# Splitting the third weight unit of the last attention projection while the queries are applied

## The reference

```python
qkv = (x @ W_qkv).reshape(b, n, 3, H, DH)
...
q_p = _phi(q, random_features)        # exp(q . features - |q|^2 / 2) / sqrt(M)
k_p = _phi(k, random_features)
kv = jnp.einsum('bhnm,bhnd->bhmd', k_p, v)
out = jnp.einsum('bhnm,bhmd->bhnd', q_p, kv)
k_sum = jnp.sum(k_p, axis=2)
normalizer = jnp.einsum('bhnm,bhm->bhn', q_p, k_sum)[..., None]
out = out / (normalizer + 1e-06)
x_attn = out_as_rows @ W_proj + b_proj
y = x + x_attn
mu = jnp.mean(y, axis=-1, keepdims=True)
var = jnp.mean(jnp.square(y - mu), axis=-1, keepdims=True)
return (y - mu) * jax.lax.rsqrt(var + LN_EPS) * gamma + beta
```

## Time and profile before

| | before |
|---|---|
| median of three runs | 2881.58 us |
| the profiled execution's own time | 2884.14 us |
| span of its instructions | 2881.9 us |
| PE busy | 2717.6 us (94% of the span) |
| DVE busy | 1397.7 us (48%) |
| ACT busy | 1144.1 us (40%) |
| POOL busy | 712.7 us (25%) |
| mean granted clock of TensorE | 0.977 of full |

### The profile page before, as it was taken

The page is one execution under the profiler, slowest core; times in us unless marked ns, Lnnn a source line. Parts: engine busy times, 40 slices in busy tenths (PEclk is TensorE's granted clock), DMA queues, the critical chain, the costliest instruction groups (busy, mean ns, idle before and its releaser), DMA issues. The chain is left out here.

```text
span 2881.9 us, 49194 instructions
## 1 busy us (share of the span) xinstructions
PE 2717.6 (94%) x20011; PEld 2474.0 (86%) x20011; DVE 1397.7 (48%) x3595; ACT 1144.1 (40%) x2131; POOL 712.7 (25%) x265
## 2 busy tenths in 40 slices
PE   9999999998678999998899999999998999999899
PEld 9999999996338988998897999999668897797799
DVE  9777465665122134558742552241664473303643
ACT  7633255651004203328631263332563442356431
POOL 0134211100002321320224343323204341113022
PEclk9999999999799999999999999999999999999999
DMA  2022231025992111221031222222002121101112
GB/s 66 12 78 81 78 105 39 18 94 198 413 397 83 61 45 44 67 81 41 12 89 39 67 67 78 78 67 77 28 1 56 50 79 43 58 24 35 34 45 71
DMA packets 169682, 223.22 MB, mean 77 GB/s; under 512 B 22051, under 2 KB 150720, under 8 KB 169209
## 3 DMA queue, kind: packets, MB, share of 16 engines
q1 hardware_dynamic: 169458, 220.07, 23.3%
HBM read 216.56 MB, written 3.48 MB: 76 GB/s over the span
## 5 line engine op out<-in xcount | busy, mean ns | idle before, releaser
L284 POOL TENSOR_TENSOR weights_r<-weights,head_weights_r 128x1536 fp32r<-128x1536 f32 (+1 forms) x78 | 278.2, 3566 | 1061.6 <-ACT head_weights_r L277 1048.2
L58 PE MATMUL ps<-weights_r,buf_r 128*125 128x256 f32 (+2 forms) x3794 | 510.7, 285 | 5.2 <-POOL weights_r L284 1.9
L284 POOL TENSOR_TENSOR weights_r<-weights,weights_r 128x1536 fp32r<-128x1536 f32 (+1 forms) x74 | 262.3, 3545 | 914.1 <-ACT weights_r L277 914.1
L58 PEld LDWEIGHTS ps<-weights_r,buf_r 128*125 128x125 f32 x3794 | 478.2, 187 | 8.3 <-issue 3.5
L58 PE MATMUL ps<-head_weights_r,buf_r 128*125 128x256 f32 (+3 forms) x2548 | 351.6, 284 | 0.0
L58 PE MATMUL ps<-xT_r,weights_r 128*128 128x376 f32 (+3 forms) x2016 | 329.9, 309 | 0.0
L58 PEld LDWEIGHTS ps<-head_weights_r,buf_r 128*125 128x125 f32 (+1 forms) x2548 | 326.0, 187 | 0.0
L58 PEld LDWEIGHTS ps<-xT_r,weights_r 128*128 128x128 f32 x2016 | 304.1, 191 | 0.0
L58 PE MATMUL ps<-weights_r,xT_r 128*125 128x256 f32 x1680 | 232.1, 282 | 1.7 <-DVE resid L2380 0.9
L277 ACT ACTIVATE head_weights_r<-weights 128x1536 fp32r<-128x1536 f32 (+1 forms) x78 | 115.9, 1486 | 270.6 <-PE ps L58 158.8
L58 PEld LDWEIGHTS ps<-weights_r,xT_r 128*125 128x125 f32 x1680 | 212.4, 186 | 3.2 <-PE ps L2311 1.4
(11 more groups left out here) (419 smaller groups left out, 4369.6 us busy)
## 6 DMA issues: line engine op xcount, KB each, us to landing
expert_regions<-in_L_ffn_w SPq DMA_DIRECT2D x64, 576.0 KB, 12.9
expert_regions<-in_L_ffn_w SPq DMA_DIRECT2D x36, 768.0 KB, 20.8
weights<-in_L_mix_fc_w SPq DMA_DIRECT2D x24, 768.0 KB, 4.5
weights<-in_L_gnn_W SPq DMA_DIRECT2D x18, 768.0 KB, 4.6
expert_regions<-in_L_ffn_w SPq DMA_DIRECT2D x24, 384.0 KB, 9.6
weights<-in_L_ffn_W SPq DMA_DIRECT2D x11, 768.0 KB, 4.8
weights<-in_L_mix_w_mapT SPq DMA_DIRECT2D x9, 768.0 KB, 4.8
weights<-in_L_gnn_W_out SPq DMA_DIRECT2D x9, 768.0 KB, 4.6
```

Source lines behind the costliest of these rows:

```text
L58: mm = net.nc.tensor.matmul(ps, net.r(stationary(s, k)), net.r(moving(m, k)), start=(n == 0 and k == 0), stop=(stop and n == 2 and k == kc ...
L284: self.nc.gpsimd.tensor_tensor(self.r(load.dst), load.dst, self.r(load.high), ALU.subtract).then_inc(self.low_made, 1)
```

## The change

The third unit's high part goes into columns 3072 to 4607 of the edge buffer, and that place counts as free from `attended` on. The split moves from `LinearResidualNorm` into `QueryApply`: ACT writes the high part just before the entry `("high", 0, 1)` of its order, and POOL makes the low part in `QueryApply.gpsimd`. `LinearResidualNorm.gpsimd` does nothing now. `queried.third` hands the load to the earlier stage.

```diff
@@ QueryApply.__init__
+        self.third = None
@@ QueryApply.scalar
         for q in self.order["act"]:
             kind, c, j = q[0], q[1], q[-1]
             ts, n = self.halves(j)
+            if q == ("high", 0, 1):
+                self.net.split_high(self.third.unit, self.third.segment)
             if kind == "phi":
@@ QueryApply
+
+    def gpsimd(self, pool):
+        self.net.split_low(self.third.unit, self.third.segment)
@@ LinearResidualNorm.scalar
         nc, done, eps = self.nc, self.net.act, self.net.eps[self.eps][:TP, :]
-        self.net.split_high(self.weights[-1].unit, self.weights[-1].segment)
         for q in self.order["act"]:
@@ LinearResidualNorm
     def gpsimd(self, pool):
-        self.net.split_low(self.weights[-1].unit, self.weights[-1].segment)
+        pass
@@ network
-    normed = LinearResidualNorm(net, XT, units, tok(G[5]), net.row(ins["L3_mix_gamma"]), R, tok(G[0]), XT, 1e-5, G[3], now(), now() + bias_out.ends() + shift.ends(),
+    normed = LinearResidualNorm(net, XT, units, tok(G[5]), net.row(ins["L3_mix_gamma"]), R, tok(G[0]), XT, 1e-5, net.spare[:, 2 * SLOT:3 * SLOT], attended, now() + bias_out.ends() + shift.ends(),
                                 tiles=queried.made, partly=queried.partly)
+    queried.third = normed.weights[-1]
```

## The result

The changed kernel takes 2867.92 us (median of four runs, 2866.37 to 2870.05), the kernel before 2881.98 us beside it (2881.34 to 2884.27). The ratio is 0.995 with a 95% interval of 0.9933 to 0.9968: faster by 14.1 us, or by 9 to 19 us.

What follows compares the result with a forecast made beforehand. PE, busy 94% of the span, bounds the kernel; its 8.2 us wait and close to 1.9 us of low clock make 10.14 us gained, 0 paid: 2881.58 to 2871.4 us, range 2868.3 to 2874.8 us (8 in 10).

Steps and rivals of the forecast that it cites:

- The hole: PE's wait before its seventh ahead block, on POOL's low part, goes; sixth chunks start 10.14 us earlier, 8.2 of it wait.
- The second term, the low clock: Behind PE's wait, 3.80 us at half clock do the work of 1.90 us; close to 1.9 us gained.
- ACT's split covered: In `QueryApply`, ACT's moved split of 1.47 us fits its idle time of 1.90 us; none on the path.
- The side remark: Without ACT's idle time in `QueryApply`, exponentials would be late by up to 1.47 us once, and PE with them.
- POOL: The low part, 3.42 us, moves behind the ten additions, from about 2650.1 to 2653.5 us; none on POOL's path.
- DVE's hold: DVE's remainder of 250 tokens in `QueryApply` is held 1.7 to 3.6 us, about 3.2, by the low part; covered.
- the additions' hold: In `QueryApply`, a DVE remainder of 375 tokens took 2.23 us in place of 0.55 beside POOL's additions: held 1.7 us.
- The rule of the lock: DVE with two SBUF inputs and POOL reading SBUF block each other fully; remainder would end at about 2653.9 us.
- The range: Whole-kernel time, 8 in 10: 2868.3 to 2874.8 us, taking in the clock's two sides and DVE's full hold.
- The clock falls elsewhere: Low-clock stretches behind the change may fall otherwise: 3.4 us better, 2868.0, or as much worse, 2874.8 us; chance 0.08.

Runs made afterwards that it cites:

- Experiment 3: The kernel before with 60 unused matmuls on PE in the hole ahead of the third unit; ratio 0.9995 (0.9985 to 1.0004).
- experiment 4: The changed kernel's new place and early mark kept, but ACT splits at the old point; ratio 1.0003 (0.9994 to 1.0012) to the kernel before.
- experiment 7: The changed kernel with a second, unused copy of the unit on ACT ahead of the split; sixth chunks 61.40 us after the start of `QueryApply`.
- Experiments 5 and 6: The changed kernel with the split two and four pairs of heads later; sixth chunks 62.70 and 61.40 us after the start of `QueryApply`.

## Why the prediction was right, and where it was wrong

- **The hole.** Right to 0.02 us: 10.14 us forecast, 10.16 us in the pair of profiles; 10.2, 10.7 and 11.0 us against the three profiles of kernels with the hole (17.36, 17.93 and 18.22, less 7.20). Experiment 3 shows the split into two terms, experiment 4 that the moment of the split is the cause.
- **The second term, the low clock.** Right in kind; 1.8, 2.4 and 2.7 us in three profiles, where the sum has 1.9 from the only one that was there. By the blocks' starts the two terms of that profile are 8.34 us (2693.20 less 2684.86) and 1.80; the forecast's 8.2 and 1.9 are rounded otherwise, with the same sum.
- **ACT's split covered.** Right: 0.52 us of the gap were left, and the exponentials wait for PE as before. The side remark that without the cover PE would be late by as much as the exponentials was wrong: with the gap overrun the exponentials started 0.75 us late, ran closer together, ended 0.23 us late, and cost PE nothing that shows (experiment 7).
- **POOL.** Right: 2644.26 us in this profile, 22.8 us after the start of `QueryApply`, where 2650.1 in the old one was 22.9.
- **DVE's hold.** Right in size (3.2 us forecast, 3.2 measured) and right that the place hides it. Experiments 5 and 6 show that this is a property of the place: it costs PE some 1.3 us two pairs later and 0.2 us four pairs later. What the forecast missed is that the additions' hold of 1.7 us, taken from the one profile that it had, is 5.2 us in two profiles of twelve. Even then PE lost only 0.2 us.
- **The rule of the lock.** The Trainium skill ("SBUF — State Buffer", section "Who interferes with whom") says that the loser blocks for the whole instruction. In all three profiles above the held DVE instruction ends 0.3 to 0.4 us after POOL's: 2647.98 and 2647.71 us, 2671.84 and 2671.56, 2684.24 and 2683.84. By that rule the cost can be estimated before the run, within 0.2 us here: the end of POOL's instruction, plus the instruction's own time. It holds for a single POOL instruction. Against the additions, which follow each other without a gap, the loser waited for one of them in ten profiles and for three in two.
- **The range: wrong.** The step that failed is the rival "The clock falls elsewhere" with its counterargument that "the three runs shown agree within 1.1 us". The prediction took the agreement of three runs for the scatter and looked for the low clock only behind the change, 3.4 us either way. The runs put single executions of the kernel before between 2876.84 and 2885.06 us (59 of them, mean 2880.90, standard deviation 2.1), and those of the changed one between 2866.37 and 2876.12 us (14, mean 2870.18, standard deviation 2.9). The difference of these means is 10.7 us, with an uncertainty of 1.6 us at 95% (two times the root of 2.9 squared over 14 plus 2.1 squared over 59). That is the sum with the average low-clock term. The first series' 14.1 us was such a mean with 3.4 us of luck. A mean of four has a standard deviation of 1.4 us on the one side and 1.1 us on the other, so their difference has 1.8 us, and 3.4 us is nearly twice that: it happens, but not often. The two medians lay apart by chance, the changed kernel's 2.3 us below its overall mean and the other's 1.1 us above. The prediction had a figure that would have warned it: it puts what a measurement can tell at 5.8 us, but its range ends 3.1 us below the forecast.

## What to carry to other kernels

A wait that stands in the chain behind the last reader of a buffer is often a wait for the place and not for the data: give the result a place that has been free for long, and then move the producer as well, since the place alone gained nothing. Put the moved work where every engine that it disturbs has idle time left before the consumer's next need, and check each bank that hangs on it; the same move two pairs of heads later cost some 1.3 us. And judge a gain of 10 us in 2900 by the stretch in the trace between two landmarks, which here repeats to 0.01 us in the changed kernel and to 0.9 us in those with the hole, before judging it by medians of a few runs, which here wander by 3 us.

## What the hardware showed that I had not expected

- Idle time of PE can be turned into clock: 60 unused matmuls in an 8.17 us hole kept the granted clock at 1.00 and gave back 1.7 to 2.5 us, 30 in a 4.45 us hole gave back 1.5 to 2.5 us of the products behind it. That the whole program gains by it is not shown.
- A DVE instruction that waits for POOL is not served next for certain. A remainder of 0.55 us that met additions of some 1.8 us, one behind the other, took 2.2 us in ten profiles and 5.8 us in two, where three additions ran before it.
- The same code, ahead of everything that was changed, took 2621.5 to 2630.1 us in twelve profiles to reach `QueryApply`; in one step of 2.5 us the granted clock was 0.93 against 1.00.
- Four exponentials that start 0.75 us late end only 0.23 us late, since they no longer wait for PE one by one (1.95 us in place of 2.47): the idle gap ahead of a group is a lower bound of the room.
